# Order of work at the head of a step on ScalarE and VectorE in a fused attention and Hadamard feed-forward kernel

## The chip, the cores and the metric

One core of a Trainium2 chip runs the whole program. The metric is the device time of one execution in microseconds (us). Six names are used for the engines: PE (TensorE, matmuls), PEld (its weight loads), DVE (VectorE), ACT (ScalarE), POOL (GpSimd) and SP (SyncE, which issues all DMAs here).

## The reference, cut to what matters

Eight sequences of 1024 tokens, 512 wide, go through an attention block and a feed-forward block:

```python
x = L0_attn_x                                   # 8 x 1024 x 512
x = x + attn(layernorm(x))                      # one latent head of 64, causal softmax, RoPE
h = silu(y @ W1.T) * (y @ W3.T)                 # y = layernorm(x), h is 2048 wide
x = x + hadamard(h) @ W2.T                      # hadamard: orthonormal Walsh-Hadamard transform
```

The transform is linear and is applied to W2 once, before the main loop.

## The kernel before, in words

**Tiling.** A sweep s (0 to 7) is the feed-forward block of one sequence, 1024 tokens. It has 16 steps h, one for each 128 hidden columns; the main loop runs over k = 16 s + h, 128 steps in all. A group of four steps makes a quarter of the hidden width; the down projection of a quarter (`down`, line 779) is spread over the four steps behind it. Beside the feed-forward steps of sweep s, the attention of sequence s + 1 runs in small pieces (as two halves a, called x blocks here, of four tiles of 128 rows). Sweep 0's sequence has its attention ahead of the loop, and sweep 7 has no attention beside it. Sweep 0 also carries the preparation of the weights (splitting W1, W3 and the transformed W2 into two float16 parts).

**Products.** Every matmul operand is split in a high and a low float16 part, so a product of two blocks takes three matmuls. In a step, TensorE makes seven products, numbered 0 to 6 (`product`, line 745), a Strassen-like scheme for the two 256-wide halves of the two weights and the tokens. The products meet in PSUM banks with the help of the other engines:

- `copy_b` (line 1126, ScalarE): once product 0 is there, bank B is copied to the other bank. Product 2 waits for it.
- `copy_p5` (line 1131, ScalarE): product 1 is copied to SBUF.
- `sum_c` (line 1725) and `sum_e` (line 1731), VectorE: sums behind products 2 and 4. Product 4 waits for `sum_c`, product 6 for `sum_e`.
- `silu` (line 1136, ScalarE) behind products 3 and 5, then `hidden` (line 1735, VectorE), which multiplies gate and linear part. The hidden product with index 0 needs product 6 and so runs at the head of the next step.
- `high` (line 1142, ScalarE) makes the high part of the step's 128x1024 hidden block as float16; `low_part` (line 1746, VectorE) subtracts it from the block for the low part. The next step's first `silu` overwrites the block and waits for both. The down projection of the quarter waits for the low part.

**The order of the work** is written out by hand, one queue for each engine. In every step there are seven fill points, `fill(k, 0)` to `fill(k, 6)`, at which each engine takes the attention piece (a slot, one for each product) that is due. In steps with k a multiple of 4, the last fill point of the step before is taken in the new step's head. Slots fall on the same step and point in each of the sweeps 1 to 6: the normalised V at point 0 of step 2 (`norm1_parts`, line 1420), the low probability part of the third tile at point 0 of step 6 (`low`, line 1486), the Newton steps of a norm at point 0 of step 7. Sweep 0 is one slot later.

**The seam between sweeps.** In a sweep's last step (h = 15, `last`) the first token blocks of the next sweep are prepared, and in a sweep's first step (h = 0, `first`) the rest: `tokens_high` (line 1111, ScalarE) makes the high part of a token block, `tokens_low` (line 1709, VectorE) the low part, `tokens_sum` (line 1713, VectorE) a difference of blocks. In step 0 the next x block also begins: `conv` splits it (line 1376, VectorE's part), and TensorE's first projection (line 529) waits for that.

The head of a step before the change, on ScalarE:

```python
if k:
    high(k - 1)
    if k % 4 == 0:
        fill(k - 1, 6)
copy_b(k)
```

Of the kernel before, what the change touches and what calls it, by code (L numbers as in the profile page):

```python
# [47 lines left out]
def slots(s, f):  # L48

    z = f - (4 if s == 0 else 3)  # L50
    return [(c, z - ODD * c) for c in range(2) if 0 <= z - ODD * c < NSLOT]
# [18 lines left out]
def tile_no(a, t):  # L70
    return 4 * a + t + 1
# [25 lines left out]
def gu_no(k, i):  # L97

    return 7 * k + i + 1
# [37 lines left out]
def build_kernel(nc, x, xT, w13, w13t, w2, small, cst, tab, wscr, w2scr, w2tmp, out):  # L137
    with ExitStack() as ctx:
# [788 lines left out]
        def _(ac):  # L927
# [77 lines left out]
            def attention(a, slot):  # L1005
                if slot < 4:
                    conv(a, slot)
                if slot == 6:
                    latent(a)
                    latent2(a)  # L1010
                if slot == 13:
                    values(a)
                if slot == 15:
                    rope_k(a)
                if slot == 16:
                    rope_q(a)
                for t in range(4):
                    at = slot - tile_slot(a, t)
                    if at == 1:
                        exps(a, t)  # L1020
                    if at == 4 + groups(a):
                        parts_o(a, t, oh, ol)
                    if slot == end_slot(a) + 5 + t:
                        xtrans(a, t)
# [58 lines left out]
            def split2(i):  # L1083
                j = SJ[i]
                w.wait_ge(p_fm, NH + i + 1)
                w.wait_ge(v_s2, 1)
                if i >= 8:
                    w.wait_ge(d_w2st[j // 4 % 2], 16)
                ac.activation(W2S[:, j // 4 % 2, j % 4, 0, :], (G, U)[i % 2], ACT.Copy, scale=afs[:, 32 + j:33 + j]).then_inc(a_w2, 1)
# [3 lines left out]
            def scale_rows(h):  # L1093
                w.wait_ge(p_wb, h + 1)
                w.wait_ge(g_wm, 2 * h)
                ac.activation(sc[:, :], (G, U, Y)[min(h, 2)][:, 0:256], ACT.Copy).then_inc(a_sc, 1)
# [29 lines left out]
            def copy_b(k):  # L1126
                w.wait_ge(p_gu, gu_no(k, 0))
                w.wait_ge(v_hA, k)
                ac.activation(PF[:, 1 - k % 2, :], PF[:, k % 2, :], ACT.Copy).then_inc(a_cb, 1)  # L1129

            def copy_p5(k):
                w.wait_ge(p_gu, gu_no(k, 1))
                w.wait_ge(v_e, k)
                ac.activation(p5[:, :], PF[:, 3, :], ACT.Copy).then_inc(a_p5, 1)  # L1134
# [7 lines left out]
            def high(k):  # L1142
                q = k // 4
                w.wait_ge(v_hA, k + 1)
                w.wait_ge(v_hE, k + 1)
                if q >= 2:
                    w.wait_ge(p_d, d_no(q - 2, 7))
                ac.activation(H[:, q % 2, k % 4, 0, :], SH[:, :, :].rearrange("p i c -> p (i c)"), ACT.Copy).then_inc(a_hi, 1)  # L1148
# [140 lines left out]
            def fill(k, j):  # L1289
                s, h = divmod(k, NH)  # L1290
                f = 7 * h + j
                if s + 1 < NS:
                    for c, slot in slots(s, f):
                        attention(2 * s + 2 + c, slot)
                if s == 0 and f in SCALE_AT:
                    scale_rows(SCALE_AT[f])
                if s == 0 and f in SPLIT_AT:
                    split2(SPLIT_AT[f])

            for k in range(NK):  # L1300
                s, h = divmod(k, NH)
                first, last = s > 0 and h == 0, s + 1 < NS and h == NH - 1
                split = s == 0 and 1 <= h < NH - 1
                if k:
                    high(k - 1)
                    if k % 4 == 0:
                        fill(k - 1, 6)
                copy_b(k)
                if k == 0:
                    for i in (1, 4, 2, 5):  # L1310
                        tokens_high(0, i)
                if first:
                    tokens_high(s, 3)
                if last:
                    tokens_high(s + 1, 0)
                if split:
                    forms_high(h + 1, 0)
                fill(k, 0)
                copy_p5(k)
                if first:  # L1320
                    tokens_high(s, 4)
                if split:
                    forms_high(h + 1, 1)
                fill(k, 1)
                if last:
                    tokens_high(s + 1, 1)
                fill(k, 2)
                if first:
                    tokens_high(s, 5)
                silu(k, 0)  # L1330
                if k == 0:
                    tokens_high(0, 6)
                fill(k, 3)
                if first:
                    tokens_high(s, 6)
                fill(k, 4)
                silu(k, 1)
                if last:
                    tokens_high(s + 1, 2)
                fill(k, 5)  # L1340
                if k % 4 < 3:
                    fill(k, 6)
# [4 lines left out]
        def _(ve):  # L1347
# [365 lines left out]
            def tokens_sum(s, i):  # L1713

                w.wait_ge(a_xn, tile_no(2 * s + 1, 3))
                w.wait_ge(v_t, 4 * s + {1: 0, 4: 1, 2: 2, 6: 3}[i])

                w.wait_ge(v_xf, xf_no(s, {1: 0, 4: 0, 2: 1, 6: 3}[i]))
                b12, b22 = (XS[:, 1, 2 * j:2 * j + 2, :].rearrange("p k c -> p (k c)") for j in range(2))
                u, v = {1: (b12, xblock(0)), 4: (b22, b12), 2: (b22, xblock(1)), 6: (xblock(3), xblock(2))}[i]  # L1720
                ve.tensor_tensor(xblock(i), u, v, ALU.subtract).then_inc(v_t, 1)
# [24 lines left out]
            def low_part(k):  # L1746
                q = k // 4
                w.wait_ge(a_hi, k + 1)
                w.wait_ge(v_hA, k + 1)
                w.wait_ge(v_hE, k + 1)  # L1750
                ve.tensor_tensor(H[:, q % 2, k % 4, 1, :], SH[:, :, :].rearrange("p i c -> p (i c)"), H[:, q % 2, k % 4, 0, :],  # L1751
                                 ALU.subtract).then_inc(v_lo, 1)
# [137 lines left out]
            def fill(k, j):  # L1890
                s, h = divmod(k, NH)
                if s + 1 < NS:
                    for c, slot in slots(s, 7 * h + j):
                        attention(2 * s + 2 + c, slot)
                f = 7 * h + j
                if s == 0:
                    if f == SUMS_AT - 2:
                        scales(4, NH, 2)
                        sums()
                    if f == SUMS_AT + 2:  # L1900
                        scale2()
                    if f in SPLIT_AT:
                        split2(SPLIT_AT[f])

            for k in range(NK):
                s, h = divmod(k, NH)
                first, last = s > 0 and h == 0, s + 1 < NS and h == NH - 1
                if k:
                    hidden(k - 1, 0)
                    if k % 4 == 0:  # L1910
                        fill(k - 1, 6)
                    low_part(k - 1)
                if first:
                    tokens_low(s, 3)
                    tokens_low(s, 4)
                fill(k, 0)
                if last:
                    tokens_low(s + 1, 0)
                    tokens_sum(s + 1, 1)
                fill(k, 1)  # L1920
                if s == 0 and 1 <= h < NH - 1:
                    forms_low(h + 1)
                if k:
                    out_rows((k - 1) // 4 - 1, 2 * ((k - 1) % 4) + 1)
                sum_c(k)
                if k == 0:
                    tokens_sum(0, 6)
                if first:
                    tokens_low(s, 5)
                    tokens_sum(s, 6)  # L1930
                if last:
                    tokens_low(s + 1, 1)
                    tokens_sum(s + 1, 4)
                fill(k, 2)
                fill(k, 3)
                sum_e(k)
                if k == 0 or first:
                    tokens_low(s, 6)
                if last:
                    tokens_sum(s + 1, 2)  # L1940
                fill(k, 4)
                hidden(k, 1)
                out_rows(k // 4 - 1, 2 * (k % 4))
                if last:
                    tokens_low(s + 1, 2)
                fill(k, 5)
                if k % 4 < 3:
                    fill(k, 6)
# [126 lines left out]
```

## Time and profile before

| what | value |
|---|---|
| median of 3 runs | 2251.51 us (2250.56 to 2254.12) |
| the profiled execution's own time | 2254.15 us |
| its span, first to last instruction | 2252.3 us |
| granted TensorE clock, mean over the span | 0.983 of full speed |
| busy: PE, DVE, ACT, POOL | 2143.6, 1448.9, 982.7, 234.1 us |

A median is compared with a median; sums over rows of the trace are made against the profiled execution. A row of the page's list of groups gives line, engine, operation, the tiles written and read, how often, busy time and mean duration, and then the idle time of the engine just before, with what ended most of it.

### The profile page before, as it was taken

How to read it: one execution, taken by the hardware profiler on the slowest of the kernel's cores; microseconds unless marked ns; L12 is line 12 of the kernel's file. 1: busy time of each engine (PE TensorE's matmuls, PEld its weight loads, DVE VectorE, ACT ScalarE, POOL GpSimd, SP SyncE). 2: the span in 40 equal slices, each digit the busy share in tenths (PEclk: the TensorE clock that was granted, in tenths of full speed). 3: DMA queues.
4: the chain of work that ended last, by engine and by line, in shares of the span. 5: the costliest groups of instructions: out<-in, count | busy, mean ns of one | idle time of the engine just before them, and what ended most of it. 6: DMA issues, size and time to landing. Idle time of an engine off the chain costs nothing. (4 is left out here: it accounts for less than half of the span.)

```text
span 2252.3 us, 27382 instructions
## 1 busy us (share of the span) xinstructions
PE 2143.6 (95%) x10108; PEld 1012.6 (45%) x10108; DVE 1448.9 (64%) x2758; ACT 982.7 (44%) x1493; POOL 234.1 (10%) x212
## 2 busy tenths in 40 slices
PE   6778899999999999999999999999999999999999
PEld 3433444444444444444444444444444444444444
DVE  7886676767657675666757675576756667563333
ACT  6855454434443534434444444435344344442221
POOL 2344554000000000000000000000000000000000
PEclk8789999999999999999999999999999999999999
DMA  8344324333233323234233332333332342323221
GB/s 330 138 146 156 123 93 130 122 108 103 91 97 120 120 101 99 88 114 140 74 107 116 116 98 87 102 115 121 100 99 94 111 137 74 105 82 112 84 85 54
DMA packets 127654, 252.97 MB, mean 112 GB/s; under 512 B 74528, under 2 KB 74656, under 8 KB 122144
## 3 DMA queue, kind: packets, MB, share of 16 engines
q1 hardware_dynamic: 127520, 251.21, 33.7%
q8 instruction: 81, 1.33, 0.2%
q14 instruction: 53, 0.43, 0.1%
HBM read 194.81 MB, written 39.85 MB: 104 GB/s over the span
## 5 line engine op out<-in xcount | busy, mean ns | idle before, releaser
L772 PE MATMUL PF<-XF,WS 128*128 128x512 f16 x1792 | 685.4, 382 | 17.8 <-ACT PF L1129 10.0
L773 PE MATMUL PF<-XF,WS 128*128 128x512 f16 x1792 | 683.1, 381 | 0.0
L774 PE MATMUL PF<-XF,WS 128*128 128x512 f16 x1792 | 682.8, 381 | 0.0
L796 PE MATMUL PD<-W2S,H 128*128 128x512 f16 x1024 | 388.6, 379 | 0.0
L797 PE MATMUL PD<-W2S,H 128*128 128x512 f16 x1024 | 388.6, 379 | 0.0
L798 PE MATMUL PD<-W2S,H 128*128 128x512 f16 x1024 | 388.6, 379 | 0.0
L1140 ACT ACTIVATE SH<-PF,afs 128x512 f32<-128x512 f32 x256 | 175.8, 687 | 378.6 <-PE PF L774 377.8
L772 PEld LDWEIGHTS PF<-XF,WS 128*128 128x128 f16 x1792 | 176.1, 98 | 245.9 <-issue 39.1
L1743 DVE SCALAR_TENSOR_TENSOR SH<-PF,afs,SH 128x512 f32<-128x512 f32 x256 | 191.8, 749 | 140.3 <-ACT SH L1140 118.1
L1148 ACT ACTIVATE H<-SH 128x1024 f16<-128x1024 f32 x128 | 135.2, 1056 | 323.9 <-DVE SH L1743 323.9
L774 PEld LDWEIGHTS PF<-XF,WS 128*128 128x128 f16 x1792 | 176.2, 98 | 214.1 <-issue 4.7
L773 PEld LDWEIGHTS PF<-XF,WS 128*128 128x128 f16 x1792 | 176.4, 98 | 179.2 <-issue 8.0
L1751 DVE TENSOR_TENSOR H<-SH,H 128x1024 f16<-128x1024 f32 x128 | 156.8, 1225 | 130.3 <-ACT H L1148 130.1
L1762 DVE SCALAR_TENSOR_TENSOR ring<-PD,afs,ring 128x512 f32<-128x512 f32 x224 | 166.8, 745 | 52.5 <-PE PD L798 52.0
L1964 POOL TENSOR_TENSOR ring<-ring,bb 128x512 f32<-128x512 f32 x56 | 70.9, 1289 | 1231.6 <-DVE st L1388 1211.7
L1733 DVE TENSOR_TENSOR PF<-PF,p 128x512 f32<-128x512 f32 x128 | 89.1, 696 | 130.6 <-PE PF L774 129.7
L796 PEld LDWEIGHTS PD<-W2S,H 128*128 128x128 f16 x1024 | 100.3, 98 | 121.2 <-issue 0.6
L798 PEld LDWEIGHTS PD<-W2S,H 128*128 128x128 f16 x1024 | 100.3, 98 | 121.2 <-issue 0.6
L797 PEld LDWEIGHTS PD<-W2S,H 128*128 128x128 f16 x1024 | 100.3, 98 | 121.1 <-issue 0.6
L1729 DVE TENSOR_TENSOR PF<-PF,p 128x512 f32<-128x512 f32 x128 | 88.8, 693 | 20.0 <-PE PF L774 18.5
L1134 ACT ACTIVATE p<-PF 128x512 f32<-128x512 f32 x128 | 75.1, 587 | 36.9 <-PE PF L774 36.9
L1129 ACT ACTIVATE PF<-PF 128x512 f32<-128x512 f32 x128 | 74.4, 581 | 26.4 <-PE PF L774 26.4
(310 smaller groups left out, 2195.8 us busy)
## 6 DMA issues: line engine op xcount, KB each, us to landing
WS<-wscr SPq DMA_DIRECT2D x112, 896.0 KB, 4.7
W2S<-w2scr SPq DMA_DIRECT2D x30, 1024.0 KB, 4.8
xraw<-xT SPq DMA_DIRECT2D x58, 256.0 KB, 3.5
ring<-x SPq DMA_DIRECT2D x56, 256.0 KB, 4.3
wscr<-WS SPq DMA_DIRECT2D x16, 896.0 KB, 4.2
out<-ring SPq DMA_DIRECT2D x56, 256.0 KB, 2.9
XF<-w SPq DMA_DIRECT2D x16, 512.0 KB, 7.5
RAW<-w13t SPq DMA_DIRECT2D x16, 512.0 KB, 4.1
```

The costliest lines, as they stand in the source:

```text
L772: pe.matmul(bank, wh, th, start=i < 2 and j == 0, stop=False, skip_group_check=True)
L773: pe.matmul(bank, wh, tl, start=False, stop=False, skip_group_check=True)
L774: m = pe.matmul(bank, wl, th, start=False, stop=j == 1, skip_group_check=True)
L796: pe.matmul(PD[:, t % 2, :], th, wh, start=j == 0, stop=False)
L797: pe.matmul(PD[:, t % 2, :], th, wl, start=False, stop=False)
L798: m = pe.matmul(PD[:, t % 2, :], tl, wh, start=False, stop=j == 3)
L1140: ac.activation(SH[:, i, :], PF[:, (1 - k % 2, 2)[i], :], ACT.Silu, scale=afs[:, k % NH:k % NH + 1]).then_inc((a_sb, a_sc2)[i], 1)
L1148: ac.activation(H[:, q % 2, k % 4, 0, :], SH[:, :, :].rearrange("p i c -> p (i c)"), ACT.Copy).then_inc(a_hi, 1)
L1733: ve.tensor_tensor(PF[:, 3, :], PF[:, k % 2, :], p5[:, :], ALU.add).then_inc(v_e, 1)
L1743: ve.scalar_tensor_tensor(SH[:, i, :], PF[:, (k % 2, 3)[i], :], afs[:, 16 + h:17 + h], SH[:, i, :], ALU.mult, ALU.mult).then_inc((v_hA, v_ ...
L1751: ve.tensor_tensor(H[:, q % 2, k % 4, 1, :], SH[:, :, :].rearrange("p i c -> p (i c)"), H[:, q % 2, k % 4, 0, :], ALU.subtract).then_inc(v ...
L1762: ve.scalar_tensor_tensor(row, PD[:, t % 2, :], afs[:, 65:66], row, ALU.mult, ALU.add).then_inc(v_ev, 1)
```

## The change

In the head of a step, ScalarE takes the last fill point of the step before (every fourth step), then `copy_b(k)`, and then `high(k - 1)`; before, `high` came first. VectorE's `low_part(k - 1)` moves behind `fill(k, 0)` and behind the token work of the seam that stands there (two `tokens_low` in step 0, one `tokens_low` and one `tokens_sum` in step 15), and ahead of `fill(k, 1)`. Nothing else is changed; the other engines' programs stay as they are.

```diff
--- before.py
+++ after.py
@@ -1301,11 +1301,11 @@
                 s, h = divmod(k, NH)
                 first, last = s > 0 and h == 0, s + 1 < NS and h == NH - 1
                 split = s == 0 and 1 <= h < NH - 1
+                if k and k % 4 == 0:
+                    fill(k - 1, 6)
+                copy_b(k)
                 if k:
                     high(k - 1)
-                    if k % 4 == 0:
-                        fill(k - 1, 6)
-                copy_b(k)
                 if k == 0:
                     for i in (1, 4, 2, 5):
                         tokens_high(0, i)
@@ -1909,7 +1909,6 @@
                     hidden(k - 1, 0)
                     if k % 4 == 0:
                         fill(k - 1, 6)
-                    low_part(k - 1)
                 if first:
                     tokens_low(s, 3)
                     tokens_low(s, 4)
@@ -1917,6 +1916,8 @@
                 if last:
                     tokens_low(s + 1, 0)
                     tokens_sum(s + 1, 1)
+                if k:
+                    low_part(k - 1)
                 fill(k, 1)
                 if s == 0 and 1 <= h < NH - 1:
                     forms_low(h + 1)
```

## Rows read from the trace of the kernel before

**Rows 1.** The page: span, TensorE's busy time, and its costliest group.

```profile
span 2252.3 us, 27382 instructions
...
PE 2143.6 (95%) x10108; PEld 1012.6 (45%) x10108; DVE 1448.9 (64%) x2758; ACT 982.7 (44%) x1493; POOL 234.1 (10%) x212
...
L772 PE MATMUL PF<-XF,WS 128*128 128x512 f16 x1792 | 685.4, 382 | 17.8 <-ACT PF L1129 10.0
```

**Rows 2.** Waits of TensorE in sweep 3: releaser, us in total, times, longest.

```profile
PE PF L772 <- ACT PF L1129: 1.3, 2, 0.8
...
PE XY L529 <- DVE Kl L1383: 1.1, 3, 0.7
...
PE XY L597 <- DMA PT<-Pl: 0.9, 2, 0.6
...
PE XY L553 <- DVE V L1432: 0.4, 1, 0.4
...
PE PF L772 <- DVE PF L1729: 0.2, 1, 0.2
```

**Rows 3.** Timelines of ScalarE, VectorE, TensorE, step 3: start, us, operation, idle before.

```profile
1001.24 1.06 ACT L1148 ACTIVATE H<-SH 128x1024 f16<-128x1024 f32 x1 [1.53 <-DVE SH L1743]
...
1002.20 0.58 ACT L1129 ACTIVATE PF<-PF 128x512 f32<-128x512 f32 x1
...
1002.33 1.22 DVE L1751 TENSOR_TENSOR H<-SH,H 128x1024 f16<-128x1024 f32 x1 [1.12 <-ACT H L1148]
...
1004.87 0.69 DVE L1729 TENSOR_TENSOR PF<-PF,p 128x512 f32<-128x512 f32 x1
...
1002.84 0.39 PE L772 MATMUL PF<-XF,WS 128*128 128x512 f16 x1 [0.78 <-ACT PF L1129]
```

**Rows 4.** The same timelines, step 15 of sweep 3.

```profile
1198.78 0.58 ACT L1129 ACTIVATE PF<-PF 128x512 f32<-128x512 f32 x1 [0.68 <-PE PF L774]
...
1199.27 1.05 ACT L1122 ACTIVATE XF<-XS 128x1024 f16<-128x1024 f32 x1
...
1198.13 1.23 DVE L1751 TENSOR_TENSOR H<-SH,H 128x1024 f16<-128x1024 f32 x1 [1.12 <-ACT H L1148]
...
1200.35 1.23 DVE L1711 TENSOR_TENSOR XF<-XS,XF 128x1024 f16<-128x1024 f32 x1 [0.99 <-ACT XF L1122]
...
1203.52 0.69 DVE L1729 TENSOR_TENSOR PF<-PF,p 128x512 f32<-128x512 f32 x1
...
1205.05 0.38 PE L772 MATMUL PF<-XF,WS 128*128 128x512 f16 x1
```

**Rows 5.** Timelines of VectorE and TensorE, step 0 of sweep 3.

```profile
956.07 0.69 DVE L1729 TENSOR_TENSOR PF<-PF,p 128x512 f32<-128x512 f32 x1
...
957.53 0.38 PE L772 MATMUL PF<-XF,WS 128*128 128x512 f16 x1
...
959.67 0.50 PE L529 MATMUL XY<-Kh,Wc 128*128 128x512 f32 x1 [0.68 <-DVE Kl L1383]
```

**Rows 6.** Timelines of VectorE and TensorE, step 2 of sweep 3.

```profile
986.85 0.43 DVE L1432 TENSOR_TENSOR V<-PB,V 128x256 f16<-128x256 f32 x1
...
987.34 0.40 PE L553 MATMUL XY<-id,V 128*128 128x128 f16 x4 [0.43 <-DVE V L1432]
```

**Rows 7.** Timelines of VectorE, GpSimd, TensorE, steps 2 and 13 of sweep 0.

```profile
166.66 0.16 DVE L1356 TENSOR_TENSOR st<-st 128x4 f32<-128x4 f32 x1
...
166.85 2.11 DVE L1358 SCALAR_TENSOR_TENSOR st<-st 128x4 f32<-128x4 f32 x1
...
377.24 3.22 DVE L1491 SCALAR_TENSOR_TENSOR Pl<-PB,Ph 128x512 f16<-128x512 f32 x2
...
166.82 2.12 POOL L1995 TENSOR_TENSOR WS<-WX,WS 128x1024 f16<-128x1024 f32 x1 [4.64 <-ACT WS L1107]
...
171.20 1.15 PE L724 MATMUL PD<-H,cst_s 128*128 128x512 f32 x1 [3.90 <-DVE W2S L1700]
...
385.61 1.07 PE L597 MATMUL XY<-PT,V 128*128 128x128 f16 x16 [1.24 <-DMA PT<-Pl]
```

## The prediction

> **What bounds the kernel now.** I read the page first, then the chain that ended last, then TensorE's waits, then the heads of single steps. TensorE is busy for 2143.6 of 2252.3 us [rows 1]. Nothing else comes near that, so the time is TensorE's work plus its idle time, and only an edit that moves one of TensorE's waits can move it. A matmul is shown at 0.38 us, yet 10,108 of them fill 2143.6 us, 0.21 us each: shown matmuls overlap, so an idle time x costs about x + 0.17 us.
>
> Sweeps 1 to 6 repeat. Sweep 3 (949 to 1211 us) stands for them: five kinds of wait, none above 1.3 us in total [rows 2]. The wait that the change aims at, product 2 for bank B's copy, is 1.3 us in two places, 0.78 of it in step 3 [rows 3]. In the whole run it is 10.0 us in 15 places [rows 1]. That caps the direct gain near 10 + 15 x 0.17 = 12.5 us.
>
> In the late steps the head is a chain. VectorE ends the hidden product, ScalarE makes the upper part and then copies B, and VectorE stands 1.12 us for the upper part before it makes the lower one [rows 3]. The change removes 0.96 us (1001.24 to 1002.20) from the way to the copy and puts other work of VectorE into the 1.12 us. It pays with an upper part that starts 0.5 us later, behind a copy of 0.58 us; where the copy waits for TensorE's product 0, the upper part now waits too.
>
> **The cost part by part.** No instruction is added or removed, and no DMA. The moved low part releases nobody on SP or GpSimd. The first fill point's probability parts do release SP's transposes, which then start earlier.
>
> *Step 15 of a sweep (a loss).* Here the copy waits for TensorE and ends at 1199.36; the upper part was made before it, for nothing. ScalarE's token copy follows at 1199.27. Now the upper part stands between: the token copy, and with it VectorE's first token difference at 1200.35, comes 0.96 us later. The low part ran at 1198.13, in time that VectorE had to spare; it moves behind the two token operations, 1.23 us less the 0.1 by which a next operation overlaps (as the copy does with the upper part, [rows 3]), 1.1. The sum for product 4 then ends 2.1 us later, 1206.3 instead of 1204.21. Product 4 starts at 1205.05 [rows 4], so TensorE stands 1.3 us. Six sweeps (1 to 6) make 7.8 us. In sweep 0 the copy is not held back by TensorE, only the 1.2 us of the low part count, and 0.8 of slack hides half: 0.6 us.
>
> *Step 0 of a sweep (a loss).* The same two terms: the upper part is put ahead of the token copies, the low part behind the second token difference. The sum that ended at 956.76 ends at 958.9; product 4 starts at 957.53: 1.3 us. VectorE is then busy without a gap up to the first difference of the next x block, for which TensorE's L529 already waits (0.68 us at 959.67) [rows 5]. So that wait ends 2.1 us later as well, and the step costs 2.1 us, seven times: 14.7 us. (In sweep 7 there is no x block; there the chain of token work holds product 6 in its place. If it doesn't, that one costs 1.4.)
>
> *Steps 2 and 3 (gains).* In step 2 the first fill point has the normalised V. It now fills the time in which VectorE waited, and L553's wait of 0.43 us goes [rows 6]: with 0.17, 0.6 us. In step 3 the copy ends 0.97 us earlier and its wait of 0.78 goes, 0.85 us with the smaller overlap of the short matmul ahead of it. What is late next is the sum for product 4: the low part ends only 0.5 us later than today and TensorE comes 1.45 us earlier, so some 0.2 us come back. Step 3 keeps 0.64.
>
> *The other steps of sweeps 1 to 6.* Step 12 holds the other copy wait (1.3 - 0.78 = 0.5 us), but right behind it TensorE waits for a transpose [rows 2] whose source was made before the head: nothing gained. Step 13 saves 0.2 (its product 2 comes 0.2 us late behind the copy, which overlapping matmuls hide from the idle column). Step 14 has no fill work to put in, its low part comes 0.5 us later, and the token norm behind it makes TensorE wait 0.2. In step 6 the third tile's low part goes ahead, so that its transposes start 2.3 us earlier; in two of the six sweeps a wait of about 0.9 us goes. In steps 1, 4, 5, 7 to 11 the slack or another wait hides everything; in step 9 only 0.1 us of slack is left. Together 6 x (0.6 + 0.64 + 0.2 - 0.2) + 1.7 = 9.1 us of gain.
>
> *Sweep 0 (a gain, the least certain term).* In step 2 VectorE's Newton steps move ahead. They were caught beside GpSimd's form difference (2.12 us): one instruction on 128x4 elements took 2.11 us, where its like take 0.16. Now they end before it, and TensorE's 3.90 us wait for the splitting ends 3.0 us earlier. In step 13 the parts of the last tile took 3.22 us beside the same GpSimd operation; they now run before it, and the waits behind, for the sum and for the transpose (1.24 us), give 2.65 us [rows 7]. Step 14 gives 1.1, step 7 0.7, step 3 0.5, steps 5 and 8 together 0.5. Step 1 loses 0.95 (its last x block is split behind the upper part), step 12 0.2. Sum: a gain of 7.3 us. Its bounds are a loss, if the low part gets caught in place of the Newton steps, and a gain of 1.12 us in each of 15 steps.
>
> The low part is the operation that moves towards GpSimd's in sweep 0, and it reads two tensors of SBUF. The Trainium skill, SBUF — State Buffer, "Who interferes with whom", says that a VectorE operation with two SBUF inputs and a GpSimd operation that reads SBUF exclude each other for a whole instruction; the 2.11 us row agrees. By that rule the edit saves the lock in two places and can meet it in others.
>
> **Sum.** 7.8 + 0.6 + 14.7 = 23.1 us lost; 9.1 + 7.3 = 16.4 gained; +6.7 us. On the profiled execution's 2254.15 us (span 2252.3 [rows 1] and 1.85 around it) this makes 2260.9. That execution is 2.6 us above the median of 2251.51, so I predict 2258.2 against the median. A measurement can tell about 0.2%, 4.5 us.
>
> **Rivals.**
> *A, faster: sweep 0 belongs to VectorE.* If each of 15 waits of 1.12 us turns into TensorE's time, and three operations of 2.1 us get out from beside GpSimd, sweep 0 gives 16.8 + 6.3 = 23.1 in place of 7.3: 2251.5 + 23.1 - 9.1 - 23.1 = 2242.4. It decides from 18.6 us there. For it: TensorE's long waits in that stretch end with VectorE [rows 7]. Against it: others end with a transpose or GpSimd, and half of the steps have no work at that fill point. 8%.
> *B, no change: the seam is cheap.* If the x block's difference at step 0 is held by its load and not by VectorE's queue, the wait that exists there (0.68 + 0.17) swallows most of the 1.3 us: 0.5 per step 0. Then 8.4 + 3.5 - 16.4 = -4.5: 2247, or 2251 if sweep 0 gives little. Against it: VectorE has no idle time ahead of that wait's end [rows 5]. 17%.
> *C, much slower: the lower part's 0.5 us reaches TensorE in every step without fill work,* 3, 9, 12, 13 and 14, in six sweeps: 14.7 us more, 2273. Against it: only steps 3 and 14 lie that close. 5%.
> *D, slower: the low part is caught beside GpSimd* in sweep 0, in some five steps at 2.1 us: 10.5 more, 2269. It is the lock's price without its gain. Above I let it fall only where it has slack. 10%.
> The forecast itself keeps 60%; its own range is 2253 to 2264 (the step-0 cost at 1.3 instead of 2.1 takes 5.6 away; half of sweep 0's gain missing adds 3.7).
>
> **Numbers.** Slower by over 0.2%: nearly all of the forecast (0.55), C and D: 0.70. Faster: A and the edge of B: 0.10. The rest, 0.20, is no change. The range of 2250 to 2267 leaves out A, C, half of D and a few points of B.
>
> **What would show it.** In sweeps 1 to 6 the waits for the copy are gone but for traces. Product 4 waits for the sum (L1729's operation) at steps 15 and 0, 1.1 us or more each, and the wait for the first x difference in step 0 stays near 0.7, but ends later. L553's wait is gone. Sweeps 1 to 6 are each some 2.2 us longer, sweep 0 some 7 us shorter, and the steps of sweep 7 but the first keep their length. I am wrong if the sum at steps 15 and 0 isn't waited for, or if sweep 0 moves by over 12 us or not at all.

## The result, and the profile after

| | before | after |
|---|---|---|
| median, both timed on one chip | 2251.82 us (2250.56 to 2254.12) | 2267.70 us (2267.51 to 2269.85) |
| the profiled execution's own time | 2254.15 us | 2267.51 us |
| its span | 2252.3 us | 2265.7 us |

The changed kernel takes 1.0072 times the time of the kernel before (95% interval 1.0054 to 1.0089), 0.7% more. The forecast of 2258.2 us had the side right and the size wrong: 2267.7 lies 0.7 us above the upper end of the range. Between the medians the time rose by 15.9 us, between the two profiled executions by 13.4, and the forecast's sum was 6.7.

The page of the kernel after: span, busy times, and the groups of TensorE's first matmuls and of the low part.

```profile
span 2265.7 us, 27412 instructions
...
PE 2141.8 (95%) x10108; PEld 1008.6 (45%) x10108; DVE 1441.0 (64%) x2758; ACT 976.6 (43%) x1493; POOL 240.7 (11%) x212
...
L772 PE MATMUL PF<-XF,WS 128*128 128x512 f16 x1792 | 684.6, 382 | 25.7 <-DVE PF L1729 21.3
...
L1751 DVE TENSOR_TENSOR H<-SH,H 128x1024 f16<-128x1024 f32 x128 | 159.9, 1249 | 153.8 <-ACT H L1148 153.3
```

TensorE does the same work (2141.8 us against 2143.6), so the loss is idle time. Its first matmuls waited 17.8 us in all, 10.0 of that for bank B's copy [rows 1]. They now wait 25.7 us, and 21.3 of it is for VectorE's `sum_c` (L1729). The copy is no longer what they wait for.

TensorE's waits in sweep 3 of the kernel after (us in total, times, longest), to be held against [rows 2]:

```profile
PE PF L772 <- DVE PF L1729: 2.8, 4, 1.2
PE XY L529 <- DVE Kl L1383: 1.7, 3, 1.3
PE XY L597 <- DMA PT<-Pl: 1.6, 2, 0.9
PE XY L616 <- DVE xs L1533: 0.8, 2, 0.6
```

The 1.3 us for the copy and the 0.4 for V are gone, as the change meant. In their place the sum costs 2.8 instead of 0.2, the x block 1.7 instead of 1.1, and a transpose 1.6 instead of 0.9.

**Step 15**, timelines of ScalarE, VectorE and TensorE (start, us, operation, idle before), against [rows 4]:

```profile
1203.02 0.58 ACT L1129 ACTIVATE PF<-PF 128x512 f32<-128x512 f32 x1 [3.29 <-PE PF L774]
1203.51 1.05 ACT L1148 ACTIVATE H<-SH 128x1024 f16<-128x1024 f32 x1
1204.46 1.05 ACT L1122 ACTIVATE XF<-XS 128x1024 f16<-128x1024 f32 x1
...
1205.54 1.23 DVE L1711 TENSOR_TENSOR XF<-XS,XF 128x1024 f16<-128x1024 f32 x1 [4.29 <-ACT XF L1122]
1208.04 1.22 DVE L1751 TENSOR_TENSOR H<-SH,H 128x1024 f16<-128x1024 f32 x1
1209.83 0.69 DVE L1729 TENSOR_TENSOR PF<-PF,p 128x512 f32<-128x512 f32 x1
...
1210.58 0.39 PE L772 MATMUL PF<-XF,WS 128*128 128x512 f16 x1 [1.12 <-DVE PF L1729]
```

ScalarE's copy stands 4.24 us later than before, which is what the work up to this step had already cost. The sum starts 6.31 us later: the step puts it back by 2.07 us. TensorE's product 4 starts 5.53 us later, so the step costs 1.29 us. VectorE's idle time of 4.29 us is where the low part used to run; the chain copy, upper part, token copy, token difference, low part, sum is now in one line.

**Step 0**, timelines of VectorE and TensorE, against [rows 5]:

```profile
961.07 0.69 DVE L1729 TENSOR_TENSOR PF<-PF,p 128x512 f32<-128x512 f32 x1
...
961.90 0.38 PE L772 MATMUL PF<-XF,WS 128*128 128x512 f16 x1 [1.16 <-DVE PF L1729]
...
964.67 0.50 PE L529 MATMUL XY<-Kh,Wc 128*128 128x512 f32 x1 [1.32 <-DVE Kl L1383]
```

TensorE's matmuls ahead of the first wait stand 3.04 us later than before. Product 4 is 4.37 later and the x block 5.00 later: 1.33 us are lost at the sum and 0.63 at the x block, whose wait grew from 0.68 to 1.32. The step's first matmul stands 2.92 us later, so another 0.12 goes ahead of product 3, and step 0 costs 2.08 us. In sweep 7, where no x block is there, step 0 costs 2.08 us as well; TensorE's timeline has the second wait at product 6:

```profile
2019.44 0.38 PE L772 MATMUL PF<-XF,WS 128*128 128x512 f16 x1 [1.16 <-DVE PF L1729]
...
2023.96 0.39 PE L772 MATMUL PF<-XF,WS 128*128 128x512 f16 x1 [0.47 <-DVE XF L1711]
```

**Steps 2 and 3**, timelines of ScalarE, VectorE and TensorE, against [rows 3, 6]:

```profile
988.89 0.58 ACT L1129 ACTIVATE PF<-PF 128x512 f32<-128x512 f32 x1 [5.33 <-DVE SH L1743]
989.49 0.43 DVE L1432 TENSOR_TENSOR V<-PB,V 128x256 f16<-128x256 f32 x1
991.74 0.39 PE L553 MATMUL XY<-id,V 128*128 128x128 f16 x4
...
1005.70 0.58 ACT L1129 ACTIVATE PF<-PF 128x512 f32<-128x512 f32 x1 [1.60 <-DVE SH L1743]
1007.39 1.23 DVE L1751 TENSOR_TENSOR H<-SH,H 128x1024 f16<-128x1024 f32 x1 [1.79 <-ACT H L1148]
1010.68 0.39 PE L772 MATMUL PF<-XF,WS 128*128 128x512 f16 x1 [0.24 <-DVE PF L1729]
```

V is ready long before L553, and product 2 waits no more. In step 3 the late low part makes product 4 wait 0.24 us through the sum, as forecast; TensorE loses 0.41 us by it (0.24 and the 0.17 of overlap), and the step keeps 0.44 of the 0.85 us that it gained at product 2.

### The profile page after: what moved, and what is told of

It is laid out like the page before. It is cut to its first block and busy times, and to the rows that moved or that the text cites. A ratio compares the mean times of both kernels' runs of the same rounds, so it can differ in the third digit from the quotient of the medians.

```text
span 2265.7 us, 27412 instructions
## 1 busy us (share of the span) xinstructions
PE 2141.8 (95%) x10108; PEld 1008.6 (45%) x10108; DVE 1441.0 (64%) x2758; ACT 976.6 (43%) x1493; POOL 240.7 (11%) x212
## 3 DMA queue, kind: packets, MB, share of 16 engines
q8 instruction: 81, 1.33, 0.2%
## 5 line engine op out<-in xcount | busy, mean ns | idle before, releaser
L772 PE MATMUL PF<-XF,WS 128*128 128x512 f16 x1792 | 684.6, 382 | 25.7 <-DVE PF L1729 21.3
L1751 DVE TENSOR_TENSOR H<-SH,H 128x1024 f16<-128x1024 f32 x128 | 159.9, 1249 | 153.8 <-ACT H L1148 153.3
L1711 DVE TENSOR_TENSOR XF<-XS,XF 128x1024 f16<-128x1024 f32 x56 | 68.2, 1220 | 57.8 <-ACT XF L1122 57.8
L1729 DVE TENSOR_TENSOR PF<-PF,p 128x512 f32<-128x512 f32 x128 | 88.4, 690 | 15.0 <-PE PF L774 15.0
```

What stands on the lines that cost most here:

```text
L772: pe.matmul(bank, wh, th, start=i < 2 and j == 0, stop=False, skip_group_check=True)
```

## The experiments

All kernels are the kernel before with two conditions put in, so that a step can take either order. A is the condition for ScalarE's new order, V the one for VectorE's:

```python
if A:                              # ScalarE
    if k % 4 == 0:
        fill(k - 1, 6)
    copy_b(k)
    high(k - 1)
else:
    ...                            # as before: high, fill, copy_b

if not V:                          # VectorE, behind hidden(k - 1, 0)
    low_part(k - 1)
...
if V:                              # behind fill(k, 0) and the token work
    low_part(k - 1)
```

With `A = V = k` (every step but the first) this is the changed kernel. VectorE's lines are 6 higher in these kernels than before (the sum is L1735, the low part L1757), GpSimd's 9. The kernels with the seam as before, with one half in all steps, and with the new order in chosen steps were timed on one chip, where the kernel before took 2251.93 us (15 runs); the seam's halves, sweep 0 and step 12 on another, where it took 2253.51 (21 runs); the two repetitions on a third, one execution each. The kernel before differs by 1.6 us between the first two chips, so a difference of medians across them can be off by that much. Where it matters, the difference to each chip's own kernel before is given too, or the shift between two traces. A step's cost in a trace is always taken at TensorE here: from the first matmul of its product 0 to that of the next step, one kernel against the other.

**The seam alone as before.**

```diff
-A = V = k
+A = V = k and not (first or last)
```

> Steps 0 (from sweep 1 on) and 15 (up to sweep 6) keep the old order on both engines, all others have the new one. Theory S (the seam): the traces put 3.4 to 3.7 us per sweep on the seam, so without it the change is a gain: each of sweeps 1 to 6 gives back about 0.7 to 0.8 us, sweep 0 about 5, 2242 to 2245 us. Rival L (the low part's 0.5 us delay costs in every step): stays above the kernel before, 2255 us or more. Rival P (transposes that wait longer at step 12, as once in the changed kernel, 3.1 us): 2245 to 2252 us, with single long waits for PT in the trace.

Measured: 2244.85 us (2243.83 to 2246.61), 0.9966 of the kernel before (0.9953 to 0.9978). The seam costs 2267.7 - 2244.85 = 22.9 us, and 23.7 between the traces (seven steps 15 at 1.30 us, seven steps 0 at 2.08); the terms of the forecast were 23.1. What the change does elsewhere is a gain, but of 7.1 us, not 16.4. The page of this kernel:

```profile
span 2242.0 us, 27412 instructions
...
L772 PE MATMUL PF<-XF,WS 128*128 128x512 f16 x1792 | 684.1, 382 | 9.4 <-DVE PF L1735 5.3
```

Of the 21.3 us that TensorE waited for the sum, 16.0 belong to steps 15 and 0.

**The seam's two halves.** First ScalarE as before there and VectorE new, then the other way round.

```diff
-A = V = k
+A = k and not (first or last); V = k
```

> The changed kernel with ScalarE's old order in steps 0 and 15 only; the low part stays late there. Theory S with the terms of the prediction (1.1 us of low part on VectorE's chain, 0.8 of slack at product 4): 0.4 a step 15, 1.1 a step 0, 11 us above the kernel with the whole seam as before: 2256 us.

```diff
-A = V = k
+A = k; V = k and not (first or last)
```

> The changed kernel with VectorE's old place of the low part in steps 0 and 15 only; ScalarE copies first there. Theory S: 0.35 a step 15, 1.0 a step 0, 9 us above the kernel with the whole seam as before: 2254 us. Each half alone costs less than half of 22.9 where slack of 0.8 hides part of it; so the two together with e5 should stay a little below it. If one half were the whole cost, it would show 2265 us or more.

Measured: 2255.84 us (2254.93 to 2257.69; ratio 1.0014, 1.0006 to 1.0023) and 2255.17 (2252.91 to 2256.22; ratio 1.0005, 0.9996 to 1.0014). Above the kernel with the whole seam as before that is 11.0 us for VectorE's half and 10.3 for ScalarE's, but on two chips: counted from each chip's kernel before it is 9.4 and 8.7, 18.1 in sum against 23.0 for both. The traces say per step: step 15 costs 0.35 us with VectorE's half and 0.36 with ScalarE's, against 1.30 with both; step 0 costs 1.21 and 0.95, against 2.08. So the halves add up at step 0 and not at step 15, where each alone is mostly hidden. Timeline of TensorE with VectorE's half alone, step 15 of sweep 2 and step 0 of sweep 3 (two lines):

```profile
941.60 0.39 PE L772 MATMUL PF<-XF,WS 128*128 128x512 f16 x1 [0.18 <-DVE PF L1735]
...
956.43 0.38 PE L772 MATMUL PF<-XF,WS 128*128 128x512 f16 x1 [0.41 <-DVE PF L1735]
...
959.20 0.50 PE L529 MATMUL XY<-Kh,Wc 128*128 128x512 f32 x1 [1.31 <-DVE Kl L1389]
```

With one half the slack ahead of product 4 takes most of the delay (0.18 and 0.41 us are left), and the x block's wait is 1.31 us already. With both halves that wait is the same (1.32), and the rest of the delay comes out at product 4. The delay of a queue was paid here at the first waits without slack, not where it arose.

**Each half of the change alone, in all steps.**

```diff
-A = V = k
+A = k; V = False
```

> ScalarE's new order alone; VectorE's low part stays where it was. Theory S: the copy waits go, but the low part now waits for the later upper part ahead of everything else on VectorE. Step 15 costs about 0.4, step 0 about 1.0, step 14 0.2, steps 2 and 3 together gain only 0.1 to 0.2: 1.2 us per sweep, and sweep 0 loses some 3: 2260 us to 2264 us. If the token copies' delay on ScalarE alone were the seam's cost, it would be 2266 us or more.

```diff
-A = V = k
+A = False; V = k
```

> VectorE's new order alone; ScalarE's stays. Theory S: the seam costs 0.35 at step 15 and 1.1 at step 0, step 2 gains 0.6, the copy waits of steps 3 and 12 stay: 0.9 us per sweep lost, sweep 0 gains some 5: 2250 to 2255 us. If the moved low part alone were the cost: 2262 us or more.

Measured: the low part moved alone gives 2252.87 us (2249.06 to 2254.18), ratio 0.9999 (0.9990 to 1.0008): no difference, as expected. The copy first alone gives 2291.55 (2290.67 to 2292.62), ratio 1.0173 (1.0159 to 1.0187). That is 40 us slower where 8 to 12 were expected, a miss of the theory behind this edit. Step by step against the trace of before it loses 12 us in sweep 0, 2.7 to 3.7 in each of the six sweeps, and 3.2 more at one place in sweep 2. Steps 15, 0 and 14 cost 0.35, 0.95 and 0.35 us, about as expected. Steps 2 and 3 were to gain 0.1 to 0.2 together and lose 0.1; steps 6, 8 and 10, which the theory had at nothing, lose up to 0.95, 0.3 and 0.6. In sweep 0 the largest losses are 2.7 us in step 1, 3.8 in step 3 and 4.0 in step 9. Two of them go with the following, in the timelines of VectorE, GpSimd and TensorE:

```profile
196.98 2.50 DVE L1476 TENSOR_TENSOR Q<-PB,Q 64x512 fp32r<-64x512 f32 x1
196.72 2.22 POOL L2004 TENSOR_TENSOR WS<-WX,WS 128x1024 f16<-128x1024 f32 x1 [13.59 <-ACT WS L1107]
199.53 0.58 PE L583 MATMUL XY<-Kh,Q 128*128 128x256 f32 x1 [3.28 <-DVE Q L1476]
...
317.21 2.50 DVE L1476 TENSOR_TENSOR Q<-PB,Q 64x512 fp32r<-64x512 f32 x1
...
319.76 0.50 PE L583 MATMUL XY<-Kh,Q 128*128 128x512 f32 x1 [2.74 <-DVE Q L1476]
```

An operation of VectorE that takes 0.69 us elsewhere took 2.50 beside GpSimd's form difference of 2.22, twice, and TensorE stood 3.28 and 2.74 us for it. The two halves are not independent: without the late low part, the copy first puts other work of VectorE into GpSimd's way at these two places (the rest of the 12 us was not taken apart), and with both halves sweep 0 gains. So the halves don't sum (+40 and +1 against +16 for both). By the traces sweep 0 gains 6.3 us with VectorE's half alone and 5.5 with both, so its gain comes from VectorE's half.

**Sweep 0 as before.**

```diff
-A = V = k
+A = V = s
```

> The old order in all of sweep 0, the new one from sweep 1 on. The gain in sweep 0 is then the difference to the changed kernel (2267.7 us). The traces say 5.5 to 6: 2273 to 2274 us. The prediction's terms say 7.3 less 0.6: 2274.4 us. If sweep 0 gave nothing: 2268 us.

Measured: 2272.84 us (2271.16 to 2273.53), ratio 1.0086 (1.0073 to 1.0100). Sweep 0's part of the change, its step 15 included, is a gain: 5.1 us against the changed kernel's median, 3.5 counted from each chip's own kernel before, and 5.5 or 3.9 in the trace of the changed kernel against the two traces of the kernel before. The forecast had 6.7. Timelines of VectorE and GpSimd in sweep 0 of the kernel after, against [rows 7]:

```profile
167.17 0.16 DVE L1358 SCALAR_TENSOR_TENSOR st<-st 128x4 f32<-128x4 f32 x1
...
170.72 2.00 DVE L1751 TENSOR_TENSOR H<-SH,H 128x1024 f16<-128x1024 f32 x1
194.04 2.00 DVE L1751 TENSOR_TENSOR H<-SH,H 128x1024 f16<-128x1024 f32 x1
207.51 2.91 DVE L1751 TENSOR_TENSOR H<-SH,H 128x1024 f16<-128x1024 f32 x1
...
169.52 2.13 POOL L1996 TENSOR_TENSOR WS<-WX,WS 128x1024 f16<-128x1024 f32 x1 [4.67 <-ACT WS L1107]
...
372.89 1.29 DVE L1491 SCALAR_TENSOR_TENSOR Pl<-PB,Ph 128x512 f16<-128x512 f32 x2 [1.26 <-ACT Ph L993]
...
375.86 2.22 POOL L1996 TENSOR_TENSOR WS<-WX,WS 128x1024 f16<-128x1024 f32 x1 [7.55 <-ACT WS L1107]
```

Both freed operations are there: the Newton step takes 0.16 us instead of 2.11, the last tile's parts 1.29 instead of 3.22. But in steps 2, 3 and 4 the low part is caught, 2.00, 2.00 and 2.91 us instead of 1.22: about 3.3 us of VectorE's time, which is the low part's growth in the page (159.9 us against 156.8). This is the lock that the forecast took from the Trainium skill (SBUF — State Buffer, "Who interferes with whom"), in both directions.

**Step 12 as before.** A single step of sweep 2 cost 3.1 us between the two profiles, and the other five sweeps lost nothing there.

```diff
-A = V = k
+A = V = k and h != 12
```

> The changed kernel with the old order in every step 12. Theory T (the earlier product 2 of step 12 gains nothing and makes one transpose of sweep 2 land late, as seen in all three kernels with the new order there and in none of the three with the old): 2264 to 2265.5 us, the wait for PT at step 12 of sweep 2 is 0.3 us instead of 2.3, the wait for the copy (0.47) is back, and nothing else moves. Rival (the long landing is chance): 2267 to 2268 us, or the long wait sits elsewhere.

Measured: 2264.70 us (2264.05 to 2268.34), ratio 1.0056 (1.0043 to 1.0068), 3.0 less than the changed kernel (4.7 less, counted from each chip's own kernel before; 2.9 less between the two traces). The place in the kernel after, timelines of SP's queue and of TensorE:

```profile
887.12 1.29 SPq L431 DMA_TRANSPOSE PT<-Pl  x1
...
891.55 1.00 PE L597 MATMUL XY<-PT,V 128*128 128x128 f16 x14 [2.33 <-DMA PT<-Pl]
```

Windows of the same stretch (us, busy time of PE, PEld, DVE, ACT and POOL with their counts, granted clock, DMA share, GB/s):

```profile
890.00:892.00 2.00, 0.45 (x8) 0.45 (x9) 0.92 (x2) 0.00 (x0) 0.00 (x0) 1.00 0.67 211
892.00:894.00 2.00, 2.00 (x14) 0.94 (x11) 0.57 (x2) 0.31 (x1) 0.00 (x0) 0.58 1.00 412
894.00:896.00 2.00, 2.00 (x7) 0.71 (x6) 0.00 (x0) 0.69 (x1) 0.00 (x0) 0.56 0.79 328
```

The same in the kernel with step 12 as before:

```profile
886.88 1.29 SPq L431 DMA_TRANSPOSE PT<-Pl  x1
...
889.91 0.95 PE L597 MATMUL XY<-PT,V 128*128 128x128 f16 x14 [0.28 <-DMA PT<-Pl]
```

The transpose is issued 3.25 us behind the step's first matmul in the one and 3.24 in the other, behind the same transfers and ahead of the same ones. In the changed kernel it lands after 4.4 us, with step 12 as before after 3.0, and the wait of 2.33 us shrinks to 0.28. So it is neither the moment of issue nor the order in SP's queue. The long wait (2.3 to 2.7 us) stands in all seven traces of kernels with the new order on ScalarE in step 12, and in none of the five that keep the old one there.

**Both kernels once more,** unaltered.

> The changed kernel once more, unaltered. Theory: the wait of 2.3 us for the third tile's transpose in step 12 of sweep 2 belongs to the new order and recurs; the time is about 2267.5 us. Rival: it was an accident of one profiled execution; then the wait at that place is 0.9 us, as in the other sweeps, and the time is near 2264.5.

> The kernel before once more, unaltered. Theory: the two transpose waits of 0.7 us in step 6 of sweeps 4 and 5 were particular to the one profiled execution, whose time lay 2.6 us above the median; without them the profiled time is 2251 to 2252.5 us. Rival: they belong to the kernel and recur, with a profiled time near 2254.

Measured: 2266.96 us and 2253.78, with 2253.41 for the kernel before beside them. The changed kernel again, TensorE's timeline:

```profile
891.74 0.95 PE L597 MATMUL XY<-PT,V 128*128 128x128 f16 x14 [2.42 <-DMA PT<-Pl]
```

and its windows behind that wait:

```profile
892.00:894.00 2.00, 2.00 (x20) 1.21 (x18) 0.58 (x2) 0.31 (x1) 0.00 (x0) 1.00 1.00 416
894.00:896.00 2.00, 2.00 (x10) 0.99 (x9) 0.23 (x1) 0.69 (x1) 0.00 (x0) 1.00 0.83 344
```

The late transpose recurs, so it belongs to the kernel. The fall of the granted clock behind it does not recur: 0.58 and 0.56 (towards the 1.2 GHz level) in the first profile, 1.00 here. With the fall the step cost 3.1 us, without it 1.5. The other five traces with the long wait agree: where the clock fell (both kernels with half of the seam, the copy first alone, sweep 0 as before) the step cost 3.2 to 3.4 us, where it did not (the seam as before) 1.7. So about half of the 3.1 us is the clock's.

The kernel before again, TensorE's timeline in step 6 of sweeps 4 and 5:

```profile
1317.03 0.62 PE L597 MATMUL XY<-PT,V 128*128 128x128 f16 x8 [0.98 <-DMA PT<-Pl]
...
1579.78 0.62 PE L597 MATMUL XY<-PT,V 128*128 128x128 f16 x8 [0.82 <-DMA PT<-Pl]
```

Here the theory fell: these waits were held to be particular to the first profile (0.75 and 0.69 us there) and to explain why it lay 2.6 us above the median. They recur, so their gain is real, and the 2.6 us are scatter. In this second trace the program is 1.5 us shorter by the end of sweep 0 than in the first: 1.0 and 1.4 us shorter in steps 3 and 6, 0.5 and 0.7 longer ahead of the loop and in step 0. Step 1 of sweep 2 is 0.8 longer. That is how far two traces of one program differ.

**The new order only where it gains.**

```diff
-A = V = k
+A = V = k and h in ((2, 3, 5, 6, 7, 13, 14) if s == 0 else (2, 3, 6, 13))
```

> The new order only where the traces show a gain: steps 2, 3, 6, 13 of sweeps 1 to 6 (and 7), and steps 2, 3, 5, 6, 7, 13, 14 of sweep 0. Theory S: as e3, and the small losses of steps 4, 5, 8, 10, 14 (0.6 us together per sweep) and of sweep 0's steps 1, 9, 11 are gone too: 2236 to 2241 us. If it is not below e3, those small losses were not the new order's.

Measured: 2237.75 us (2236.57 to 2239.78), ratio 0.9937 (0.9923 to 0.9950): faster than both kernels, 14 us below the one before and 30 below the changed one. Its page:

```profile
span 2235.0 us, 27390 instructions
...
L772 PE MATMUL PF<-XF,WS 128*128 128x512 f16 x1792 | 683.5, 381 | 11.7 <-DVE PF L1735 4.6
```

TensorE's first matmuls wait more here than in the kernel with only the seam as before (11.7 us against 9.4; the copy waits of step 12 are back), and it is 7.1 us faster all the same. Between the two traces it gains 2.1 us in the steps 14 of six sweeps, 0.9 in their steps 5 and 9, 1.7 in step 12 of sweep 2 and 2.4 in sweep 0.

## Why the prediction was right on the side and wrong on the size

The cost of each step at TensorE (from the first matmul of its product 0 to that of the next step, after against before, both profiled executions; sweep 0 with what stands ahead of it) gives the account, in us:

| part | predicted | measured |
|---|---|---|
| seam, sweeps 1 to 6 (step 14: 0.2, 15: 1.3, 0: 2.1 each) | +21.6 | +22.3 |
| step 0 of sweep 7 | +2.1 | +2.1 |
| sweeps 1 to 6, steps 1 to 13, without the next row | -10.3 | -8.5 |
| step 12 of sweep 2 | 0 | +3.1 |
| sweep 0 | -6.7 | -5.5 |
| sum, before rounding | +6.7 | +13.4 |

**The steps that failed** are four. Step 12 was priced at "nothing gained" and cost 3.1 us. The hidden steps and step 3 made the gain of the six sweeps 8.5 us instead of 10.3. Sweep 0 gave 5.5 for 6.7. And 2.6 us were taken off the sum for a difference that was scatter.

**The seam: right, term by term.** TensorE's costs in one seam are 0.34 (step 14), 1.30 (step 15) and 2.08 us (step 0), 3.7 in all for 3.6. Step 14, forecast at 0.2, makes the 0.7 us of difference. The sum came 2.07 us later for 2.1. The text's remark that the x block's wait "stays near 0.7" was wrong beside its own arithmetic: product 4 loses 1.3 and VectorE is late by 2.1, so the wait had to grow by the difference, and did. In sweep 7 the chain of token work holds product 6 in the x block's place (0.47 us of wait), and the step costs the same 2.08 us, as the text had it.

**Steps 1 to 13 of the six sweeps: gains mis-sized.** Step 2 gave 0.60 for 0.6, step 13 0.20 for 0.2. Step 3 gave 0.44 for 0.64: the text took off 0.2 for product 4's wait, which was 0.24 and by its own rule costs 0.17 more. Step 6 gave 1.9 us in all for 1.7. The line "in steps 1, 4, 5, 7 to 11 the slack or another wait hides everything" failed for two of them: step 5 loses 0.06 us and step 9 0.08 in each sweep, 0.8 together; the others stay within 0.02. These and step 3's 1.2 us make the miss.

**Step 12: the wait that the text didn't price.** It said "nothing gained", and in five sweeps that holds: the wait for the copy, 0.5 us, turned into a longer wait for the transpose. In sweep 2 the transpose itself landed late, 3.1 us with the clock's fall in the profiled execution. Nothing in the trace of before shows this. It is the largest single part of the miss.

**Sweep 0: near in the sum, but by errors that cancel.** Steps 13 and 14 gave 5.0 us for 3.75, all of the surplus in step 14 (2.7 for 1.1). Up to step 12 the gain was 1.7 for 3.55, and against the second trace of the kernel before only 0.2. Step 2 gave its 2.9 for 3.0. Step 1 lost 2.4 us (2.7 against the second trace) and not 0.95: TensorE's wait for its last x block grew from 1.62 to 3.55 us. Steps 5 and 8 lost 0.5 where they were to give 0.5, and step 6's 1.3 us lie within what two traces of the same program differ by. Step 15 cost 1.30 us, not 0.6: product 4 waits 1.13 us there, as in the other sweeps, where the text let only a part of the delay count. TensorE's waits of step 1, before and after:

```profile
146.44 0.50 PE L529 MATMUL XY<-Kh,Wc 128*128 128x512 f32 x1 [1.62 <-DVE Kl L1383]
...
147.27 0.50 PE L529 MATMUL XY<-Kh,Wc 128*128 128x512 f32 x1 [3.55 <-DVE Kl L1383]
```

**From the sum to the median.** The text took off 2.6 us because the profiled execution lay that far above the median. Medians of the kernel before were 2251.82, 2251.93 and 2253.51 in three comparisons, single executions of it 2253.41 and 2253.78 in the last. The 2.6 us were scatter of executions and chips. With them the distance is complete: 6.7 us in the terms, 2.6 here, and 0.2 by which the changed kernel's median lies above its own profiled execution, 9.5 in all.

**The rivals.** A (sweep 0 gives 23 us) is out: it gave 3.5 to 5.5. B (the seam is cheap) is out: 22.9. C (0.5 us in each of five steps) is out: step 14 loses 0.34, step 9 0.08, and steps 3, 12 and 13 lose nothing but for step 12 of sweep 2. D named 2269, near the result, and that is luck: it had the low part caught in some five steps of sweep 0, at 2.1 us each. It was caught in three, 3.3 us of VectorE's time in all, and sweep 0 still gained; the miss lies mostly elsewhere. What the three places cost TensorE was not measured. **Still open** is why the transpose of step 12 lands 1.4 us late in one sweep of six: the link to ScalarE's order is shown, the mechanism is not.

## What to carry to other kernels

Price a reordering where two queues already run without slack, here the seam: an operation moved behind a chain of another engine costs its length less the slack behind it, in every repetition (2.1 us of delay cost 1.30 us at step 15, with 0.8 of slack, and 2.08 at step 0), and it can be left as it was in just those steps. A local condition on the step (2237.75 us) turned a loss of 0.7% into a gain of 0.6%. The halves of a change that meet in one queue need not sum. And before a term is taken from one trace, it is worth knowing what two traces of the same program differ by.

## What the runs showed of the hardware

- A VectorE operation that starts beside GpSimd's 128x1024 difference (2.1 to 2.2 us) takes about the rest of that one and then its own length: 0.16 us became 2.11, 0.69 became 2.50, and 1.22 became 2.00 or 2.91, the longer the earlier it started beside GpSimd's (at 207.51 us, GpSimd's at 207.20 for 2.13). The Trainium skill (SBUF — State Buffer, "Who interferes with whom") states the exclusion, and the rows agree. What had not been expected is how a change in one queue moves it from victim to victim.
- A transpose issued at the same place of the same step in two kernels landed after 3.0 and after 4.4 us. In all seven traces with ScalarE's new order in step 12 TensorE waited 2.3 to 2.7 us for it there.
- TensorE stood idle for 2.33 us in one execution and for 2.42 in another at the same place. Behind the first the granted clock was 0.58 and 0.56 for 4 us, behind the second 1.00, a difference of 1.6 us. In seven traces the idle time at this place was 2.33 to 2.65 us, and the clock fell behind it in five (2.33, 2.48, 2.50, 2.64 and 2.65 us) and not in two (2.42 and 2.64). The length of the idle time alone did not decide.
